# An adaLN block with a mixture of experts: expert weights split inside their ring slots, a reordered hand-over between two stages, and gathers held at tile 8

## The reference

```
mod = silu(c) @ wmod                        # six rows of 512 per batch
h   = layernorm(x) * (1 + ca) + sa
x   = x + ga * RWKV(h)                      # time mix: K, V, R, O products; channel mix:
                                            # kk = xk @ Wkey.T (512 -> 2048), silu, @ Wval.T, gated by sigmoid(xr @ Wcr.T)
h5  = layernorm(x) * (1 + cb) + sb
shared = gelu(h5 @ Wsh_up) @ Wsh_down       # for every token, 512 -> 512 -> 512
probs  = softmax(h5 @ W_router)             # 16 experts, the best two of each token
routed = sum over the two: gelu(h5 @ Wrt_up[e]) * gate @ Wrt_down[e]     # 512 -> 256 -> 512
out = x + gb * (shared + routed)
```

## Time and profile before

| what | us |
|---|---|
| median of 3 runs (lowest to highest) | 1007.43 (1007.05 to 1010.03) |
| the profiled execution, its own time | 1009.81 |
| its span, first to last instruction | 1008.1 |
| PE busy in the span | 910.2 (90%) |
| DVE busy | 561.5 (56%) |
| ACT busy | 381.6 (38%) |
| POOL busy | 383.7 (38%) |

### The profile page before, as it was taken

How to read it: one execution, slowest core, us unless ns; L and a number is a source line. 1 busy time by engine, 2 the same in 40 slices (tenths; PEclk the granted TensorE clock), 3 DMA queues, 4 the chain that set the end, 5 groups by cost and what they waited for, 6 DMA issues and landing times.

```text
span 1008.1 us, 13848 instructions
## 1 busy us (share of the span) xinstructions
PE 910.2 (90%) x4264; PEld 728.5 (72%) x4265; DVE 561.5 (56%) x995; ACT 381.6 (38%) x630; POOL 383.7 (38%) x296
## 2 busy tenths in 40 slices
PE   7897879999989999999998999999938999999973
PEld 2466768788768888878887888787827777777742
DVE  5896988985854112651355154419593444444638
ACT  2664564765645333212321232254402333332421
POOL 3332100100024454172046004564366888870660
PEclk9899889999989999999999999999977999999967
DMA  9558567653354352341153016347635766774763
GB/s 356 168 164 254 166 220 241 188 188 104 105 176 158 105 178 94 114 149 72 39 173 129 26 55 207 107 155 201 209 112 182 254 227 222 227 241 136 211 189 112
DMA packets 108225, 166.70 MB, mean 165 GB/s; under 512 B 8440, under 2 KB 53496, under 8 KB 107408
## 3 DMA queue, kind: packets, MB, share of 16 engines
q1 hardware_dynamic: 61200, 113.64, 33.8%
q0 software_dynamic: 9824, 33.56, 10.5%
q10 hardware_dynamic: 37152, 18.88, 6.3%
HBM read 98.63 MB, written 67.42 MB: 165 GB/s over the span
## 4 chain that ended last, share of the span: by engine, by line
PE 70%; DVE 16%; issue 6%; DMA 4%; ACT 3%; POOL 1%; SPq 1%; DVEq 0%; ACTq 0%; POOLq 0%
PE kk_ps L419 5%; PE kk_ps L421 5%; PE kk_ps L420 5%; PE kv_ps L419 5%; PE kv_ps L421 5%; PE kv_ps L420 5%; PE mm_ps L419 4%; PE mm_ps L420 4%; PE mm_ps L421 4%; PE up_ps L419 4%; PE dn_ps L419 3%; PE up_ps L420 3%; PE up_ps L421 3%; PE dn_ps L421 3%; PE dn_ps L420 3%
## 5 line engine op out<-in xcount | busy, mean ns | idle before, releaser
L1541 DVE TENSOR_TENSOR silu<-kk_ps,silu 128x512 fp32r<-128x512 f32 x64 | 44.2, 691 | 206.2 <-ACT silu L2148 188.3
L2144 ACT ACTIVATE kk_ps<-kk_ps 128x512 f32<-128x512 f32 x64 | 37.2, 582 | 212.8 <-PE kk_ps L421 200.1
L419 PE MATMUL kk_ps<-xk,cm_w 128*128 128x512 f32 x256 | 101.0, 394 | 0.0
L419 PE MATMUL kv_ps<-cm_w,silu 128*128 128x512 f32 x256 | 100.6, 393 | 0.0
L421 PE MATMUL kk_ps<-xk,cm_w 128*128 128x512 f32 x256 | 99.8, 390 | 0.0
L421 PE MATMUL kv_ps<-cm_w,silu 128*128 128x512 f32 x256 | 99.7, 390 | 0.0
L420 PE MATMUL kk_ps<-xk,cm_w 128*128 128x512 f32 x256 | 99.6, 389 | 0.0
L420 PE MATMUL kv_ps<-cm_w,silu 128*128 128x512 f32 x256 | 99.6, 389 | 0.0
L1844 DVE TENSOR_TENSOR xsT<-xs_ps,xsT 128x512 fp32r<-128x512 f32 x42 | 29.1, 692 | 85.1 <-ACT xsT L2235 84.8
L2325 POOL TENSOR_TENSOR rs<-mv,neghalf 128x4 f32<-128x4 f32 x12 | 14.0, 1164 | 160.6 <-DVE mv L1270 160.5
L2318 POOL TENSOR_TENSOR cm_w<-stage,cm_w 128x1024 fp32r<-128x1024 f32 x16 | 38.6, 2425 | 91.3 <-ACT cm_w L1935 91.3
(11 more groups left out here) (280 smaller groups left out, 2382.2 us busy)
## 6 DMA issues: line engine op xcount, KB each, us to landing
xs_s<-zero ACTq DMA_DIRECT2D x13, 1024.0 KB, 6.1
stage<-in_wex POOLq DMA_DIRECT2D x26, 512.0 KB
xsb<-xs_s SPq DMA_DIRECT2D x44, 256.0 KB, 2.9
ys_s<-ysb SPq DMA_DIRECT2D x41, 256.0 KB, 2.2
stage<-in_wcm SPq DMA_DIRECT2D x16, 512.0 KB, 4.1
wmod<-in_wmod SPq DMA_DIRECT2D x6, 1024.0 KB, 11.6
stage<-in_wtm SPq DMA_DIRECT2D x10, 512.0 KB, 6.4
ys_s<-zero ACTq DMA_DIRECT2D x5, 1024.0 KB, 5.4
```

What stands on the lines that cost most here:

```text
L419: pe.matmul(out, lhs[0], rhs[0], start=first, stop=False)
L1541: dve.tensor_tensor(silu[:, g % NSILU, 1, :], kk_ps[g % 2][:, :], silu[:, g % NSILU, 0, :].bitcast(F32), ALU.subtract).then_inc(s_silo, 1)
L2144: act.activation(kk_ps[g % 2][:, :], kk_ps[g % 2][:, :], ACT.Silu).then_inc(s_silu, 1)
```

## The change

The weights of the shared expert and of four experts (`PRE = 4`) are loaded whole, 1 MB per DMA, into the low half of their own slot (`ex_raw`), rounded from there by ACT and subtracted in place by POOL; `stage` isn't used for them, so the last batch's h5 rows lie in `stage` and not in `h5l`. The orders on PE, DVE, ACT and POOL in the hand-over change. On DVE and SP the first seven pairs of the loop are written out (`PEEL = 7`), and behind each DVE pair stand two adds or two `ht_lo`, or `gates_b`. The x4 rows of tiles 2 to 7 are loaded after the first four `xs` tiles, and `load_ht(3)` after the seventh pair. Gathers from tile 8 on wait for the first quarter of the last `shared_up`. PE's and ACT's loops stay loops from 0.

```diff
-PRE = 3
+PRE = 4
+PEEL = 7
+        ex_raw = sbuf(overlay, "ex_raw", [P, BASE + PRE, 2, UNIT])
 # ex_free(): one more entry, for expert 3
-                    (s_kv, last + 12)]
+                    (s_kv, last + 12), (s_kk, last + 16)]
 # SP
+            def load_unit(u):
+                sp.wait_ge(*ex_free()[u])
+                sp.dma_start(ex_raw[:, u, 1], wex_d[u]).then_inc(s_wmod[u], 16)
 # load_x4
-                        sp.wait_ge(s_kk, NB * MF)
-                    if t == TT:
                         sp.wait_ge(s_xklo, NB * KT)
-                    if t == TT + 2:
-                        sp.wait_ge(s_x4, NT)
+                    if t == 2:
+                        sp.wait_ge(s_dn, SB * TT)
             load_gb(0)
-            scatters_landed(NB - 2)
-            load_half(26, ex_half(26))
-            load_half(27, ex_half(27))
+            for u in range(4):
+                load_unit(u)
             load_ht(0)
-            for n in range(28, 34):
-                load_half(n, ex_half(n))
-            load_ht(1)
+            load_unit(4)
+            load_unit(5)
             last = NT - TT
             store_x4(last)
+            load_ht(1)
...
-            load_x4(range(TT))
+            load_x4(range(2))
...
-            load_x4(range(TT, SB * TT))
-            load_half(34, ex_half(34))
-            load_half(35, ex_half(35))
             load_gb(1)
...
             load_xs(3, 1, 2)
-            load_ht(NB - 1)
-            pairs = sp.value_load(...)
-            with sp.Fori(0, pairs) as i:
+            load_x4(range(2, SB * TT))
...
+            for i in range(PEEL):
+                pair(i)
+            sp.wait_ge(s_base, SB * TT)
+            load_ht(NB - 1)
+            pairs = sp.value_load(...)
+            with sp.Fori(PEEL, pairs) as i:
+                pair(i)
 # PE
-            shared_down(0, [0], every)
+            shared_down(0, [0], [0, 1])
             router(last + 2)
             turn5(last + 3)
-            shared_down(0, [1], [0, 1])
+            shared_down(0, [0], [2, 3])
             router(last + 3)
-            shared_down(0, [1], [2, 3])
-            shared_down(0, [2], every)
+            shared_down(0, [1], every)
+            shared_down(0, [2], [0, 1])
+            prefix_sums(NB - 1)
+            shared_down(0, [2], [2, 3])
             shared_down(0, [3], every)
-            prefix_sums(NB - 1)
             shared_up(1)
-            shared_down(1, [0, 1], first)
-            shared_down(1, [0, 1], rest)
-            shared_down(1, [2], every)
+            shared_down(1, [0], first)
             table_row()
-            shared_down(1, [3], every)
+            shared_down(1, [0], rest)
+            shared_down(1, [1, 2, 3], every)
 # DVE
-            ht_lo(1, range(KT))
+            ht_lo(1, [0, 1])
             route(NB - 1)
+            gb_shared(0)
+            ht_lo(1, [2])
             place_a(NB - 1)
             place_b(NB - 1)
+            ht_lo(1, [3])
+            gates_a()
+            table_a()
+            table_b()
+            table_c()
+            gb_shared(1)
             mid_lo(4)
-            gb_shared(0)
+            gb_shared(2)
             mid_lo(5)
-            gb_shared(1)
-            gb_shared(2)
+            gb_shared(3)
             mid_lo(6)
-            gb_shared(3)
-            table_a()
             mid_lo(7)
-            table_b()
-            ht_lo(2, range(KT))
-            table_c()
-            gb_shared(4)
-            gates_a()
-            gb_shared(5)
             table_d()
-            base_add(0)
...
-                base_add(t)
-            gates_b()
+                gb_shared(t)
+            def beside(i):
+
+                if i < 2:
+                    ht_lo(2, [2 * i, 2 * i + 1])
+                elif i < 6:
+                    base_add(2 * i - 4)
+                    base_add(2 * i - 3)
+                else:
+                    gates_b()
+
+            for i in range(PEEL):
+                pair(i)
+                beside(i)
+            with dve.Fori(PEEL, pairs) as i:
+                pair(i)
 # ACT: weight_hi(26..33) at steps m = 9 to 12 of the last batch, ht_hi(0) at 13, 34 and 35 at 15; then
-            weight_hi(31)
             gelu(0, [0])
-            weight_hi(32)
+            weight_hi(36)
             gelu(0, [1])
-            weight_hi(33)
             to_h5T(last)
-            ht_hi(1)
+            weight_hi(37)
             gelu(0, [2])
             to_h5T(last + 1)
             gelu(0, [3])
             to_h5T(last + 2)
+            ht_hi(1, [0, 1])
             to_h5T(last + 3)
+            ht_hi(1, [2, 3])
             ht_hi(2)
-            gelu(1, [0])
...
             act.wait_ge(s_sub, 1)
             act.activation(pr[:, :, :], pr[:, :, :], ACT.Exp).then_inc(s_exp, 1)
+            gelu(1)
 # POOL
-            weight_lo(26)
-            weight_lo(27)
+            for n in range(26, 34):
+                weight_lo(n)
             ht_lo(0)
...
             scatters(NB - 1)
-            weight_lo(34)
-            weight_lo(35)
+            weight_lo(36)
+            weight_lo(37)
 # expert_load: the first waits for the last scatters, which read stage
+                elif n == 0:
+                    for i in range(TT):
+                        pool.wait_ge(s_scat[i], 32 * NB)
 # gathers
                 if t >= NG:
                     pool.wait_ge(s_o1, t - NG + 1)
+                if t == NG:
+                    pool.wait_ge(s_up, (NB - 1) * KT + 1)
```

More of the change, by code:

```diff
@@ L440, in cm_half, with ex_part @@
             return wcm_d[n // 2, :, (n % 2) * HALF:(n % 2 + 1) * HALF]
-        def ex_half(n):
-            n -= 26
-            return wex_d[n // 2, :, (n % 2) * HALF:(n % 2 + 1) * HALF]
+        def ex_part(n, i, rows=None):
+            u, k0 = (n - 26) // 2, (n % 2) * KT // 2
+            rows = ex_w if rows is None else rows
+            return rows[:, u, i].rearrange("p (k c) -> p k c", c=H)[:, k0:k0 + KT // 2, :]
         def h5_row(t):
             j = t % TT
-            if t >= NT - TT:
-                return h5l[:, j]
             return stage[:, j // 2, (j % 2) * H:(j % 2 + 1) * H]
@@ L460, in x4_of @@
         def x4_of(t):
-            return x4h[:, t] if t < TT else x4m[:, t - TT] if t < TT + 2 else x4n[:, t - TT - 2]
+            return x4m[:, t] if t < 2 else x4r[:, t - 2]
         def gathered(t):
@@ L842, in _, with pair @@
             load_xs(3, 1, 2)
-            load_ht(NB - 1)
-            pairs = sp.value_load(tend[0:1, NE:NE + 1], min_val=NE // 2, max_val=NS // 2)
-            with sp.Fori(0, pairs) as i:
+            load_x4(range(2, SB * TT))
+            def pair(i):
                 load_xs(i * 2 + 4, 0, i * 2 + 3)
@@ L1745, in gates_b @@
                 done(dve.reciprocal(gates[:, 0], tops[:, :]))
-                done(dve.tensor_tensor(gates[:, 1].rearrange("p (t a) -> p t a", a=1), pr[:, :, NE:NE + 1],
-                                       gates[:, 0].rearrange("p (t a) -> p t a", a=1), ALU.mult))
+                dve.tensor_tensor(gates[:, 1].rearrange("p (t a) -> p t a", a=1), pr[:, :, NE:NE + 1],
+                                  gates[:, 0].rearrange("p (t a) -> p t a", a=1), ALU.mult).then_inc(s_gates, 1)
             def table_a():
@@ L1865, in _, with pair @@
             pairs = dve.value_load(tend[0:1, NE:NE + 1], min_val=NE // 2, max_val=NS // 2)
-            with dve.Fori(0, pairs) as i:
+            def pair(i):
                 turned_lo(0, i * 2 + 3)
@@ L1921, in weight_hi @@
             def weight_hi(n):
+                if n >= 26:
+                    act.wait_ge(s_wmod[(n - 26) // 2], 32)
+                    act.activation(ex_part(n, 0), ex_part(n, 1, ex_raw), ACT.Copy).then_inc(s_whi, 1)
+                    return
                 act.wait_ge(s_stage[n % 2], 16 * (n // 2 + 1))
@@ L2181, in _ @@
                     xk_hi(b + 1, [2, 3])
-                if b == NB - 1 and m == 11:
-                    weight_hi(26)
-                    weight_hi(27)
-                if b == NB - 1 and m == 12:
-                    ht_hi(0, [0, 1])
+                if b == NB - 1 and m in (9, 10, 11, 12):
+                    weight_hi(26 + 2 * (m - 9))
+                    weight_hi(27 + 2 * (m - 9))
                 if b == NB - 1 and m == 13:
-                    ht_hi(0, [2, 3])
-                    weight_hi(28)
-                if b == NB - 1 and m == 14:
-                    weight_hi(29)
+                    ht_hi(0)
                 if b == NB - 1 and m == 15:
-                    weight_hi(30)
+                    weight_hi(34)
+                    weight_hi(35)
             def gelu(b, tiles=range(KT)):
@@ L2400, in ht_lo @@
                                        ALU.subtract).then_inc(s_htlo, 1)
-            weight_lo(26)
-            weight_lo(27)
+            for n in range(26, 34):
+                weight_lo(n)
             ht_lo(0)
-            weight_lo(28)
-            weight_lo(29)
-            weight_lo(30)
-            post_rsqrt(NT - 4)
```

(15 more changed lines are left out.)

51 lines of the change are left out of this document (19 added, 32 removed).

## The result

The changed kernel takes 983.86 us (median of four runs, 978.6 to 985.02), the kernel before, measured beside it, 1007.24 us: a ratio of 0.9755, with an interval of 0.9714 to 0.9796. The profiled execution took 983.62 us with a span of 981.8, against 1009.81 and 1008.1. The forecast was 984. The total came out, but two of its terms did not: the gain ahead of the loop and the loss in it were both forecast too large, and the errors nearly cancelled. That the median lies 0.1 us from the forecast is luck.

What follows compares the result with a forecast made beforehand. PE was taken as near full except for two holes, before the loop and in the last shared_up. 1009.81 - 21.1 + 9 + 1 - 12.6 = 986.1, less the profiled run's 2.4 over the median: 984 us, range 970 to 1000.

Steps and rivals of the forecast that it cites:

- the gain ahead of the loop: Everything up to the loop's third `up`, forecast at 748.6 for 769.66: 21.1 us gained in all.
- the loss in it: In the loop: 9 us lost to adds beside POOL's work and 1 us to the x4 loads.
- Step 1: Up to batch 1's last shared tile: router wait gone, a new gelu wait, PE through at 736.9 for 739.09, 2.2 us gained.
- Step 2: Hole before the first `up` shrinks from 19.67 to 3.0 us, 16.7 gained; half-clock stretch behind it, another 2.2.
- the prediction's sign: Listed evidence for being right, before the loop: `up` of the first tile by 741.
- Steps 3 and 4: Loop: adds beside POOL cost 9 us; six x4 loads ahead of `load_xs(4)` cost 1 us.
- The room of 2.85 us per pair: In the loop: DVE's free time per pair, from a pair's end at 782.70 until `turned_lo` must be done by 786.29.
- The rival with hidden adds: In the loop: POOL mostly waits for PE at its start, so adds cost 1 us; total 976, chance 0.10.
- Step 5: Last `shared_up`: holding gathers from tile 8 on makes it 14.8 us instead of 27.4, 12.6 us gained.
- the last `shared_up` sets the end: Tail of the kernel before: DVE's 22.7 us of closing work hang on it, though DVE ends the chain.
- step 3: First seven pairs: two adds take 4.3 us beside POOL, 1.5 over the room, six pairs, 9 us lost.
- the 2.4 us that I took off: Whole kernel: profiled execution stood 2.4 us over the median, so 986.1 became 984 us.

Runs made afterwards that it cites:

- Experiment 8: Changed kernel with the twelve operations and gates_b put back ahead of the first turned_lo, x4 loads ahead of load_xs(2): 993.85 us, ratio 0.9829.
- experiment 9: Changed kernel with DVE's combines of tiles 5 and 6 and ACT's scaling ahead of the last shared_up's first low part: 979.39 us, ratio 0.9702.
- experiment 7: Changed kernel with eleven useless matmuls in the first pairs' waits, to keep PE at work: 986.13 us, ratio 0.977.
- experiment 5: Changed kernel with the 4 ht_lo and 8 base_add beside the first pairs left out, so output is incomplete: 982.28 us, ratio 0.9724.
- experiment 1: Changed kernel without the wait that holds the gathers from tile 8 on: 997.62 us, ratio 0.9895.
- experiment 3: Changed kernel with the hold two tiles earlier, gathers waiting from tile 6 on: 982.55 us, ratio 0.9723.
- experiment 4: Changed kernel without the hold and with 32 useless transposes ahead of all PE work: 1003.22 us, one run.
- experiment 6: Changed kernel with gelu(1) ahead of Exp on ACT and mid_lo(4) ahead of table_b on DVE: 984.77 us, ratio 0.9746.
- experiment 10: Changed kernel without the hold at tile 8, but no gather issued before the third shared_up is through: 1004.44 us, one run.
- experiment 11: Changed kernel with hold at tile 6, gelu and its low part ahead of Exp and table scan, tile 5's combine early: 979.32 us, ratio 0.9693.
- experiment 2: Kernel before with only the hold on gathers from tile 8 added: 996.24 us, ratio 0.9874.

## Why the prediction was right

**Step 1, up to the end of `shared_down(1)`: forecast 2.2 us gained, measured 0.5 lost** (739.57 for 739.09). The mechanism held: the wait at the second router product is gone, and PE waits in `shared_up(1)` for a low part (1.81 us for the 2.6 forecast), which stood behind the table work more than behind Exp. Two things make up the difference. First, "PE leaves `last_values` at 684.4 either way": it left at 685.79, 1.4 us later, but the new weight work didn't do this. The first router product of batch 2, ahead of every edit, was already 1.5 us later, at 616.52 for 615.03, and in ten profiles of kernels that are the same up to there it lies anywhere between 613.10 and 616.64. Second, and this term was mis-sized, `shared_up(1)` was forecast at 13.6 us, a wait and then full clock, and took 14.8: after the wait PE ran partly at half clock, 1.6 us more. I had counted such a dip behind the old 1.75 us wait and none behind the new one.

**Step 2, the hole: forecast 3.0 us, measured 3.15.** Experiment 8 shows the cause: with the twelve operations back the hole is 16.2 us. The first `up` came at 742.72, not by 741 as the prediction's sign had it, by what step 1 left. The pairs after it were forecast at 8.7 us, with one dip of the clock, and took 10.54; 8.25 and 8.26 at full clock (experiments 9 and 7). Again the half clock lasted longer than I allowed. The third `up` came 4.7 us later than forecast, 753.26 for 748.6, by these terms.

**Steps 3 and 4, the adds and the x4 loads in the loop: forecast 10 us, measured 3.9**, of which the adds 3.3 (experiment 5). The room of 2.85 us per pair was right: pairs with 1.28 us of adds held no `up` up, those with 3.12 left PE idle for 0.37, and those with 4.30 did hold it up, by 1.44 and 1.61, about 4.30 - 2.85. The step that failed is "the first of two adds meets it at random while the second finds POOL's next one just started: ... 4.3 us ... six pairs". It was so in two pairs of six. Not POOL's share of busy time was wrong: it is 52.8 of 76.7 us in the first pairs, 69%, and was 94.2 of 130, 72%. Wrong was "at random". POOL waits for PE's `down` time and again, so its operations and the pairs keep step, and the adds meet the same thing every third pair. From POOL's timeline (the adds start at 757.78, 767.52 and 775.66):

```profile
756.86 1.89 POOL L2444 TENSOR_TENSOR ex_w<-stage,zero 128x1024 fp32r<-128x1024 f32 x1 [10.72 <-PE dn_ps L420]
758.82 2.71 POOL L2446 TENSOR_TENSOR ex_w<-stage,ex_w 128x1024 fp32r<-128x1024 f32 x1
771.08 1.89 POOL L2444 TENSOR_TENSOR ex_w<-stage,zero 128x1024 fp32r<-128x1024 f32 x1 [3.11 <-PE dn_ps L420]
776.31 1.91 POOL L2444 TENSOR_TENSOR ex_w<-stage,zero 128x1024 fp32r<-128x1024 f32 x1
```

The first pair's adds start inside the first operation and meet both (4.30 us), the second's fall where POOL has no such operation and then waits 3.11 us for PE (1.28), and of the third's the second one meets the operation at 776.31 (3.12). Then it starts over. The same six values, 4.3, 1.3, 3.1, 4.3, 1.3, 3.1, stand in the profiles of experiments 1, 3, 4, 6, 9, 10 and 11, so this is how the kernel runs and no accident of one execution.

The rival with hidden adds named POOL's waits for PE, at 1 us; the truth lay between. The price of a meeting was as forecast: two adds that take 1.3 us alone took up to 4.3 beside POOL. That agrees with the Trainium skill, SBUF — State Buffer, "SBUF: two separate sides", by which DVE and GpSimd take a shared pair of ports for a whole instruction each.

**Step 5, the hold: forecast 12.6 us, measured 13.8 in the tail**, and 14 by experiment 1. The last `shared_up` took 13.86 us for the 14.8 forecast, with four gaps. I had taken slow matmuls as 0.70 us apart; the earlier trace rows has 20 in 18.40 us, 0.92 each, and the term came out because they were so for 3.6 us of the last `shared_up` and not for 5. The hold is released when PE has its first column, and the eight tiles behind it are no burden:

```profile
942.65 1.15 POOL L2482 DMA_INDIRECT g2b<-ys_s,pos  x1 [0.30 <-issue]
947.29 0.95 POOL L2482 DMA_INDIRECT g1b<-ys_s,pos  x1 [3.50 <-PE up_ps L420]
```

By the Trainium skill, SBUF — State Buffer, "SBUF: two separate sides", a DMA and a compute operation can't slow each other and PE never waits on anyone, by which the hold should give nothing. The traces disagree by 14 us: there is some link between the gathers and PE, whose mechanism they don't show. That "the last `shared_up` sets the end" held up to this change only. DVE's wait for its first gelu is now the last idle time of any length in the tail,

```profile
947.80 0.69 DVE L1718 TENSOR_TENSOR ht<-up_ps,ht 128x512 fp32r<-128x512 f32 x1 [4.82 <-ACT ht L2217]
```

and behind it DVE works without a pause to 979.38. Gains of 2 to 3 us ahead of the tail (experiments 5, 6, 7) are not seen at the end because their tails, from the last tile's `down` on, take 69 to 70 us, where the changed kernel's profile and that of experiment 9 take 64. In them the slow matmuls begin 13 to 17 matmuls earlier, in `shared_down(2)`, and DVE then waits 9.7 to 10.0 us for the last `shared_up`, for 4.8. Why they begin earlier isn't known. Where they don't, in experiment 9, a lead of 7.7 us reached the end whole.

**The sum.** Forecast -21.1 + 10 - 12.6 = -23.7; measured -16.4 + 3.9 - 13.8 = -26.3 in the profiled runs, and -23.4 in the medians. The gain ahead of the loop was forecast 4.7 us too high, the loss in the loop 6.1 us too high, and the tail's gain 1.2 too low. In step 3 the mechanism was right and its count wrong, so the forecast hit through errors of opposite sign, and the last 2.6 us were covered by the 2.4 us that I took off for the profiled execution's place above its median. That correction doesn't hold up: in the three later groups of timings the kernel before has medians of 1009.5 to 1010.3, as high as that execution.

**Open.** What makes PE slow. Shown: it needs the gathers (the slow pace ends with their first row, and a pause in the row removes most of it), it isn't tied to a place in the code, and a full row of gathers beside a full PE is not enough (experiments 2 and 10). One rival wasn't settled. In the eleven profiles with slow matmuls the first of them comes 20.7 to 23.5 us after the first matmul of `shared_up(2)`, and one transfer on the queue named `instruction` comes 1 to 7 us ahead of it (at 948 to 949 in the kernel before, 936 to 937 in the changed one). The same transfer stands in experiments 10 and 11 (at 942 and 934) with no slow stretch behind it, so alone it isn't enough either. In experiment 10 the row of gathers was 11 us old when it came, for 13 to 15 in the eleven, and in experiment 11 the gathers paused soon after it, so the two together may be what it takes. No experiment tried just that.

## What to carry to other kernels

Work of DVE that POOL holds up was far cheaper in the gaps of the loop (3 us) than in front of it (13), though in two gaps of six it overran the room. Size such a cost by where the other engine stands when the work starts, iteration by iteration, and not by its share of busy time: two engines that wait for the same third one keep step. Here that was 3.3 us for the 9 forecast. Where a stretch of slow matmuls has no releaser, try to pause the traffic beside it before explaining it: two lines gave 14 of 23 us here. And look at an untouched part of two profiles before you explain a difference of 2 us between them: here it differed by 3.5 us from one execution to another.

## What the runs showed of the hardware that I had not expected

The granted clock after a short wait is not the same from one execution to the next. After the same 1.81 us wait in the same program the next 25 matmuls took 7.36 us at a granted clock of 0.77 in one and 5.74 at 1.00 in another (experiment 9), and the first two pairs 10.54 or 8.25 us, with 9.47 in experiment 3. Together that is 4 us of an execution's time, about half of what the runs of one kernel differ here (975.5 to 982.9 in six), so a single profile doesn't price a dip.

DVE and POOL, both with their operands in SBUF, wait for whole operations of each other: six pairs of adds took 1.28, 3.12 or 4.30 us, with nothing between these values, and POOL's second operation took 2.71 us for 2.38 where one of these fell beside it.
